# Sixteen expert blocks beside the last batches, with experts in the order of their rows

## What is computed

```python
scores = softmax(xt @ Wg.T)
# the best 2 of 4 groups of 4 experts, then the best 4 experts within them
h = silu(einsum('td,eid->eti', xt, W1)) * einsum('td,eid->eti', xt, W3)
y = einsum('etd,te->td', einsum('eti,edi->etd', h, W2), combine)
z = (silu(xt @ Ws1.T) * (xt @ Ws3.T)) @ Ws2.T
```

## Time and profile before

| | us |
|---|---|
| median of 3 runs | 927.99 |
| profiled execution | 926.76 |
| its span | 924.9 |
| TensorE busy | 774.2 (84%) |
| VectorE busy | 738.9 (80%) |
| GpSimd busy | 517.4 (56%) |
| ScalarE busy | 483.2 (52%) |

### The profile page before, as it was taken

The page is one execution under the profiler, slowest core; times in us unless marked ns, Lnnn a source line. Parts: engine busy times, 40 slices in busy tenths (PEclk is TensorE's granted clock), DMA queues, the critical chain, the costliest instruction groups (busy, mean ns, idle before and its releaser), DMA issues.

```text
span 924.9 us, 20989 instructions
## 1 busy us (share of the span) xinstructions
PE 774.2 (84%) x6103; PEld 692.3 (75%) x6103; DVE 738.9 (80%) x2558; ACT 483.2 (52%) x1236; POOL 517.4 (56%) x512
## 2 busy tenths in 40 slices
PE   3668999999999999999988663899999999999600
PEld 3556788878788878887876552799999999999600
DVE  4556789889998899889967774898888888888534
ACT  4244565645454555555545432666666666666400
POOL 4123334656555655655545473577777777777600
PEclk9779999999999999999999865999999999999855
DMA  3656674567655765567521664978888888888598
GB/s 120 156 145 162 185 195 125 184 193 227 153 185 182 222 170 181 174 193 203 138 77 62 223 242 143 263 149 137 139 139 135 141 137 140 136 136 141 72 377 348
DMA packets 111998, 157.90 MB, mean 171 GB/s; under 512 B 13072, under 2 KB 94992, under 8 KB 111888
## 3 DMA queue, kind: packets, MB, share of 16 engines
q1 hardware_dynamic: 84000, 115.52, 43.0%
q0 software_dynamic: 26736, 36.85, 23.3%
q10 hardware_dynamic: 1152, 4.19, 1.1%
HBM read 74.55 MB, written 81.43 MB: 169 GB/s over the span
## 4 chain that ended last, share of the span: by engine, by line
PE 54%; DVE 22%; issue 9%; DMA 7%; SPq 3%; ACT 2%; POOL 2%; another core or an unknown queue 0%; DVEq 0%; POOLq 0%; ACTq 0%
PE bank L570 25%; PE bank L827 8%; DVE row_max L1121 4%; PE bank L610 4%; PE bank L794 3%; PE bank L614 3%; PE bank L654 3%; DMA acc<-acc_scr 2%; PE bank L638 2%; SPq L551 2%; DMA acc_scr<-yb,token 2%; DVE ropeds_lo L1067 2%; DVE rope_b L1107 2%; PE bank L577 2%; DVE wexp L1067 2%
## 5 line engine op out<-in xcount | busy, mean ns | idle before, releaser
L1534 POOL DMA_INDIRECT acc_scr<-yb,token x143 | 226.3, 1582 | 83.0 <-DMA acc_scr<-yb,token 36.9
L1503 POOL DMA_INDIRECT rows_scr<-xn,rows_of x128 | 128.4, 1003 | 61.9 <-issue 31.1
L570 PE MATMUL bank<-wexp,xbT_hi 128*128 x572 | 151.6, 347 | 4.9 <-DVE xbT_lo L1067 4.3
L1121 DVE TENSOR_REDUCE row_max<-bank 128x2 f32<-128x512 f32 (+1 forms) x192 | 128.9, 682 | 25.9 <-PE bank L614 24.9
L907 ACT ACTIVATE probs<-bank 128x512 f32<-128x512 f32 x192 | 110.7, 607 | 38.9 <-PE bank L654 30.8
L827 PE MATMUL bank<-wexp,upT 112*128 (+1 forms) x572 | 121.5, 305 | 0.3 <-DVE upT L1067 0.2
L610 PE MATMUL bank<-kst,qst 112*128 112x256 f32 (+1 forms) x512 | 98.8, 299 | 23.9 <-DMA kst<-qk_scr 18.8
L610 PEld LDWEIGHTS bank<-kst,qst 112*128 112x128 f32 x512 | 79.4, 199 | 38.8 <-DMA kst<-qk_scr 20.1
L1483 POOL TENSOR_SCALAR_AFFINE_SELECT probs<-probs 128x1024 f32<-128x1024 f32 x64 | 70.2, 1097 | 67.1 <-ACT probs L907 65.9
L570 PEld LDWEIGHTS bank<-wexp,xbT_hi 128*128 128x128 f32 x572 | 94.5, 192 | 7.8 <-issue 7.7
L654 PE MATMUL bank<-qst,kst 114*128 114x512 f32 (+1 forms) x256 | 84.1, 391 | 14.6 <-issue 9.3
(11 more groups left out here) (201 smaller groups left out, 2252.5 us busy)
## 6 DMA issues: line engine op xcount, KB each, us to landing
xb<-rows_scr SPq DMA_DIRECT2D x143, 138.0 KB
qk_scr<-ropeds_hi SPq DMA_DIRECT2D x64, 256.0 KB, 2.5
qst<-qk_scr SPq DMA_DIRECT2D x64, 192.0 KB
kst<-qk_scr SPq DMA_DIRECT2D x64, 192.0 KB
acc<-acc_scr SPq DMA_DIRECT2D x24, 512.0 KB, 14.5
st<-in_wexp SPq DMA_DIRECT2D x16, 608.0 KB
qk_scr<-ropeds_lo SPq DMA_DIRECT2D x32, 256.0 KB, 2.9
acc_scr<-zero SPq DMA_DIRECT2D x10, 768.0 KB
```

The lines of the kernel that those rows point to most:

```text
L570: ins = e.matmul(region, stationary(s, k), moving(m, k), start=(j == 0), stop=(j == n - 1), skip_group_check=True)
L1121: e.tensor_reduce(row_max[:, half, h:h + n, i], view, AX.X, ALU.max).then_inc(s_max)
L1503: e.indirect_dma_start(rows_scr[:, :], bass.IndirectOffsetOnAxis(ap=rows_of[b % 2][:, i, r:r + 1].bitcast(U32), axis=0), x2[:, i, :], None ...
L1534: e.indirect_dma_start(acc_scr[j % NACC][:, :], bass.IndirectOffsetOnAxis(ap=token[j % NW][:].bitcast(U32), axis=0), yb[j % NYB][:], None, ...
```

## The change

The first 16 blocks no longer wait for the list. After batch 12 (ORDER_AT) 13 x 256 x 4 picks have been made, so the expert with most rows has at least 832 of them and thereby six full blocks, the next at least five, then three and two, whatever the data: SURE = [6, 5, 3, 2], AHEAD = 16. A new stage `order` ranks the experts by their counts after batch 12. It has two trips to TensorE and 12 small VectorE instructions, and gives tables `at_slot` (which expert stands in slot x), `slot_row` (where its rows begin) and `slot_w` (where its weights begin). Weights are loaded and kept in this order, so for the 16 blocks the place of the weights in SBUF is known when the program is written, and only row and weight addresses are read from registers, on SyncE.

A new stage `ahead` holds 16 slots of five steps each, which `plan()` lays between the steps of `shared` and `route` of batches 13 to 15. In the resulting order slot 0 begins just before step 20 of batch 15's `mix`, slot 9 ends about where batch 15's `rows_of` are computed (route 23), and slot 15 ends with the tables. GpSimd's add of block j stands in slot j + 6, so two adds (blocks 4 and 5) stand between the eight scatters of batch 15, and ten in all within the stage. When `attend` of batch 15 is done, its three banks join the five. TensorE, ScalarE and VectorE run the same functions for a block as before, now taken step by step.

The list `tables` makes has 127 entries (LISTED) instead of 143. It subtracts what is sure and maps slots to experts, with one more matmul at step 2, one more at step 5 and some more VectorE arithmetic. All 16 tails are cleared in steps 3 to 6 of `tables`, ahead of the first load of the list. Stage `experts` now has four experts and begins at step 10 of `mix` 15 with four loads at once, instead of seven from step 0 on; the other twelve, 24 halves, stand at every third block from 16 to 85, and their loads go out during slots 4 to 7 and then once per six blocks, from block 26 to 68. `st` and `wexp` lie at the end of part two's memory. The adds to `chosen` move from GpSimd to VectorE (route 21 and 22). The start of `tables` and SOONER are shifted.

The core of the diff:

```diff
-SOONER = {"route": [-0.15, -0.3, -0.45]}
+SOONER = {"route": [-0.14, -0.28, -0.42], "shared": [0, 0.0, 0.3]}
...
-    runs += [[B - 1 + 5.2, 0.700 / 8, "tables", B - 1, 8], [0, 0.6 / 10, "load_wqkv", 0, 7], [0.1, 3.4 / 19, "setup", 0, 19],
-             [B - 1 + 2.799, 3.12 / 60, "experts", 0, 1000]]
+    runs += [[B - 1 + 5.46, 1.200 / 8, "tables", B - 1, 8], [0, 0.6 / 10, "load_wqkv", 0, 7], [0.1, 3.4 / 19, "setup", 0, 19],
+             [B - 1 + 2.38, 1.4 / EXPERT_STEPS, "experts", 0, EXPERT_STEPS],
+             [ORDER_AT + 6.1, 0.25 / 6, "order", 0, 6],
+             [B - 1 + 3.77, 2.73 / (5 * AHEAD), "ahead", 0, 5 * AHEAD]]
...
-ON_ATTEND = 7
-EXPERT_STEPS = 5 * ON_ATTEND
-
-BETWEEN = [(h * (E - 1) // (2 * (E - ON_ATTEND)), ON_ATTEND + h // 2, h % 2) for h in range(2 * (E - ON_ATTEND))]
+ORDER_AT = 12
+SURE = [-(-((ORDER_AT + 1) * S * (TOPK - x)) // (E - x)) // P for x in range(TOPK)]
+SLOT_OF = [x for x in range(TOPK) for _ in range(SURE[x])]
+AHEAD = len(SLOT_OF)
+LISTED = NBLK - AHEAD
+EXPERT_STEPS = 5 * TOPK
+BETWEEN = [(AHEAD + 3 * h, TOPK + h // 2, h % 2) for h in range(2 * (E - TOPK))]
...
+            def behind_attention(w):
+                w.wait_ge(s_pv, 4 * B)
+                w.wait_ge(s_oT, 4 * B)
+                w.wait_ge(s_causal, 4 * B)
+                w.wait_ge(s_max, 2 * UNITS * B)
+                w.wait_ge(s_nmax, 2 * B)
...
             def load_expert(x):
                 w.wait_ge(s_wexp, 2 * (x - NST + 1))
-                e.dma_start(st[x % NST][:], a["wexp"][x]).then_inc(d_w[x % NST], 16)
+                w.wait_ge(s_order, ORDERED)
+                at = e.value_load(slot_w[0:1, x:x + 1], min_val=0, max_val=(E - 1) * P)
+                e.dma_start(st[x % NST][:], a["wexp"][bass.ds(at, P), :]).then_inc(d_w[x % NST], 16)
...
+            def load_rows(j):
+                if j < AHEAD:
+                    x = SLOT_OF[j]
+                    w.wait_ge(s_order, ORDERED)
+                    at = e.value_load(slot_row[0:1, x:x + 1], min_val=0, max_val=(E - 1) * CAP)
+                    at = at + (j - SLOT_OF.index(x)) * P
+                    for i in range(NXN):
+                        w.wait_ge(d_rows[i], 128 * len(range(i, ORDER_AT + 1, NXN)))
+                else:
+                    w.wait_ge(s_tab, TAB_ROW)
+                    at = e.value_load(row_t[0:1, j - AHEAD:j - AHEAD + 1], min_val=0, max_val=E * CAP - P)
+                    w.wait_ge(d_tail, 16 * E)
+                    for i in range(NXN):
+                        w.wait_ge(d_rows[i], 128 * (B // NXN))
+                w.wait_ge(s_xb_turned, j - NXB + 1)
+                w.wait_ge(s_picked, j - NXB + 1)
+                e.dma_start(xb[j % NXB][:], rows_scr[bass.ds(at, P), :]).then_inc(d_xb[j % NXB], 16)
...
+            def ahead(k):
+                s, k = divmod(k, 5)
+                if k == 0:
+                    if s == 0:
+                        behind_attention(w)
+                    for j in range(4 if s else 0, 5):
+                        if s + j < AHEAD:
+                            load_rows(s + j)
+                    if 4 <= s < 4 + TOPK:
+                        load_expert(NST + s - 4)
...
+            def block_step(s, k):
+                if k == 0 and s < NBLK:
+                    turn_rows(s)
+                elif k == 1 and 0 <= s - 1 < NBLK:
+                    hidden(s - 1)
+                elif k == 2 and 0 <= s - 2 < NBLK:
+                    turn_hidden(s - 2)
+                elif k == 3 and 0 <= s - 3 < NBLK:
+                    result(s - 3)
...
-            fetch_weights(0)
-            for s in range(NBLK + 3):
...
+            fetch_weights(AHEAD)
+            for s in range(AHEAD, NBLK + 3):
+                for k in range(4):
+                    block_step(s, k)
...
+                elif stage == "ahead":
+                    if k == 0:
+                        w.wait_ge(d_zero, 16 * len(ZEROS))
+                        for i in range(2):
+                            w.wait_ge(d_base[i], 16 * len(range(i, ORDER_AT + 1, 2)))
+                    if k % 5 == 4 and k // 5 >= 6:
+                        add(k // 5 - 6)
...
-            for j in range(NBLK):
...
+            for j in range(AHEAD - 6, NBLK):
+                add(j)
```

More of the change, by code:

```diff
@@ L54 @@
 NXB, NYB, NST, NW = 6, 6, 4, 10
-NTAIL = 4
 NF, TF = 8, 4
@@ L97 @@
     "route": {20: ["rank"]},
+    "order": {0: ["od"]},
+    "tables": {0: ["cb"], 5: ["eb"]},
+    "ahead": {n: u for s in range(18) for n, u in ((5 * s, [f"x{s}"]), (5 * s + 1, [f"h{s - 1}"] if s > 0 else []),
+                                                  (5 * s + 2, [f"t{s - 2}"] if s > 1 else []),
+                                                  (5 * s + 3, [f"y{s - 3}"] if s > 2 else []))},
 }
@@ L106 @@
     "route": {21: ["rank"]},
+    "order": {5: ["od"]},
+    "tables": {5: ["cb"]},
+    "ahead": {n: u for s in range(18) for n, u in ((5 * s + 2, [f"x{s}"]), (5 * s + 3, [f"h{s - 1}"] if s > 0 else []),
+                                                  (5 * s + 4, [f"t{s - 2}"] if s > 1 else []),
+                                                  (5 * s + 5, [f"y{s - 3}"] if s > 2 else []))},
 }
@@ L125, in plan @@
             continue
-        if stage == "experts":
-            if ("attend", B - 1) not in done:
-                continue
+        if stage in ("experts", "ahead", "tables") and ("attend", B - 1) not in done:
+            continue
+        if stage in ("experts", "ahead") and k == 0 and ("order", 0) not in done:
+            continue
+        if stage == "order" and k == 0 and ("ranks", ORDER_AT) not in done:
+            continue
         if stage == "tables" and k == 0 and ("ranks", B - 1) not in done:
@@ L142, in plan @@
             done.add(("ranks", b))
[L143 removed]
+        if run[6] == n:
             done.add((stage, b))
             live.remove(run)
+        if (stage, b, k) == ("attend", B - 1, n - 1):
+            idle += [5, 6, 7]
+            last[5:] = [("attend", b, "scores"), ("attend", b, "scores"), ("attend", b, "out")]
     return order, bank, last
[L150 to L153 removed]
+ORDER_AT = 12
[3 more added lines that the diff above has]
+LISTED = NBLK - AHEAD
+FIRST = [-(-x * (ORDER_AT + 1) * S * TOPK // (E * P)) for x in range(E)]
+EXPERT_STEPS = 5 * TOPK
+BEHIND = 7
+BETWEEN = [(AHEAD + 3 * h, TOPK + h // 2, h % 2) for h in range(2 * (E - TOPK))]
+assert all(FIRST[x] > at for at, x, _ in BETWEEN)
 def layer_kernel(nc, a, out):
@@ L511, in sync_program @@
                     find_tails()
-                    zero_tail(0)
-                    zero_tail(1)
+                elif stage == "tables" and k in (3, 4, 5, 6):
+                    for x in range(4 * (k - 3), 4 * (k - 2)):
+                        zero_tail(x)
+                elif stage == "ahead":
+                    ahead(k)
                 elif stage == "load":
@@ new lines, in tensor_program, with fetch_weights, weights @@
+            at = {}
+            def fetch_weights(j):
+                w.wait_ge(s_tab, TAB_OFF)
+                last = min(j + LOADS, NBLK)
+                for i, reg in enumerate(load_registers(e, "offset", off_t[0:1, j - AHEAD:last - AHEAD])):
+                    at[j + i] = e.snap(reg, min_val=0, max_val=(E - 1) * 2 * WE)
+            def weights(j, m, first, n, rows):
+                if j < AHEAD:
+                    first += (2 * SLOT_OF[j] + m) * WE
+                    return wexp[0:rows, first:first + n]
+                return wexp[0:rows, bass.ds(at[j] + m * WE + first, n)]
@@ new lines, in turn_hidden, with result @@
+            def turn_hidden(j):
+                ps = free_block_bank(w, "t", j, s_upT, j - 1)
+                w.wait_ge(s_up, j + 1)
+                e.transpose(ps[:, 0:P], up[j % 2][:, 0:P], ident[:])
+                e.transpose(ps[:, P:2 * P], up[j % 2][:, IA:IA + 2 * IB], ident[:]).then_inc(s_up_turned)
+            def result(j):
+                ps = free_block_bank(w, "y", j, s_yb, j - 1)
+                w.wait_ge(s_upT, j + 1)
+                hi, lo = upT[j % 2], upT_lo[j % 2]
+                first = [weights(j, m, KT * SI, D, IA) for m in range(2)]
+                rest = [weights(j, m, KT * SI + D, D, P) for m in range(2)]
+                parts = ((hi[0:IA, 0, :], first[0]), (hi[0:IA, 0, :], first[1]), (lo[:], first[0]),
+                         (hi[:, 1, :], rest[0]), (hi[:, 1, :], rest[1]))
+                for n, (left, right) in enumerate(parts):
+                    ins = e.matmul(ps[:, 0:D], left, right, start=n == 0, stop=n == len(parts) - 1,
+                                   skip_group_check=True)
+                ins.then_inc(s_y)
```

501 lines of the change are left out of this document (281 added, 220 removed).

## The result

Four runs of each kernel, on one chip: 940.72 us median after (939.37 to 942.97) against 927.32 before (926.09 to 928.92). **The ratio is 1.0146, 95% interval 1.0117 to 1.0175: 13 us slower where 18 us faster were forecast.** The profiled execution took 939.58 us beside a span of 937.8.

A forecast was written before the change was run, and what follows sets the result against it. Bound: the last batch's chain of small steps, then 2.00 us of TensorE per block left. Block 16 turned at 588 instead of 613, less 7 of extras, gains 18 us: 910 us (903 to 917), range 895 to 925.

The forecast's parts named there:

- e: Extra time in the 126 loop slots after block 16 beyond 2.00 us each, from halves and adds: 7 us.
- 0.15 us a half: Delay taken for each of 24 halves at every third block, 16 to 85: 3.6 us in all.
- the sum: Gain counted from block 16's first transposition to block 142's: 613 - 588 - 7 = 18 us.
- The last x2T: Batch 15's last x2T_lo moves from 533.4 to about 529.4: fewer halves and no weight wait, less the experts' ordering.
- From there to the row numbers: Last x2T_lo to batch 15's row numbers: 33.9 us of VectorE work packed to 0.88 gives 38.5, ready at 568.
- a trough longer than summed: Sign that the forecast is wrong: batch 15's row numbers come beyond 575 us.
- Scatters last, two adds between them, clears under them: After the row numbers: GpSimd's scatters and two adds end at 583, hiding 9 us of clears; rows there at 587.
- Table loads: ScalarE's Silu ahead of batch 15's Exp adds at least two table switches, 2.6 us, mostly covered: 1 us taken.
- X: Start of block 16's first transposition on TensorE, forecast at 588 us.
- The adds, put at 3: GpSimd's adds start the loop six blocks late; the backlog makes TensorE wait 3 us (0 to 25).
- The slower rival: Adds become the loop's bound at 2.43 us each while halves and loads run: 8 us more, 936 us; chance 0.06.
- the blocks ahead only lengthen the trough: Rival: batch 15's chain waits in every queue behind block work, 928 us, no change; chance 0.04.

The follow-up runs named there:

- e9: The kernel before, unedited, on the third chip: 911.82 us, ratio 1.0009 to the kernel before.
- e10: The changed kernel, unedited, on the third chip: 906.07 us, ratio 0.9941 to the kernel before.
- e5: The changed kernel, unedited, on the second chip: 906.84 us, ratio 0.9957 to the kernel before.
- e13: The changed kernel, unedited, on the fourth chip: 907.51 us, ratio 0.9963 to the kernel before.
- e11: Changed kernel with the first eight weight splits three steps later, loads unmoved: 910.39 us, ratio 0.9979 to the kernel before.
- e7: Changed kernel with late blocks, close tables and seven experts, not four, split before the loop: 907.78 us, ratio 0.9961 to the kernel before.
- e16: Changed kernel with late blocks, close tables, seven experts split before the loop, and loop halves cut in two: 900.62 us, ratio 0.9899 to the kernel before.
- e4: Changed kernel with Tanh in place of Silu in the sixteen blocks ahead: 931.19 us, ratio 1.0088 to the kernel before.
- e3: Changed kernel without the loop's 24 halves and their weight loads, all listed blocks using slot 0's weights: 920.11 us, ratio 0.9970 to the kernel before.
- e1: Changed kernel with all steps of the sixteen blocks ahead ordered behind the last batch's ranks: 924.15 us, ratio 1.0006 to the kernel before.
- e2: Changed kernel with the eight tables steps closer together, ahead of most of the last ten block slots: 928.62 us, ratio 1.0062 to the kernel before.
- e8: Changed kernel without nine of eleven TensorE products in each of the sixteen blocks ahead: 903.54 us, ratio 0.9924 to the kernel before.
- e14: Changed kernel without nine of eleven products per block ahead, on the fourth chip: 904.85 us, ratio 0.9945 to the kernel before.
- e17: Changed kernel without nine of eleven products per block ahead, on the fifth chip: 905.46 us, ratio 0.9938 to the kernel before.
- The best form: Changed kernel with loop halves cut in two in neighbouring slots and tables closer together: 897.42 us, ratio 0.9862 to the kernel before.
- e18: Changed kernel with loop halves cut in two and closer tables, on the fifth chip: 898.89 us, ratio 0.9853 to the kernel before.

## Why the prediction was wrong, step by step

Two steps failed. The row numbers were summed with VectorE packed to 0.88 on the way there; it reached 0.63 in the record, where TensorE's results were told late, and 0.80 without that. And e was put at 7 with 0.15 us a half, where it was 12.5 and about 0.5. The term for the last x2T_lo failed too, and is smaller.

The pair e9 and e10 splits the 31.4 us: 11.9 belong to the sum (18 against 6.1), 19.5 to what differed on the chip of the result. Each side is one profile. The unedited changed kernel had its last x2T_lo at 522.31, 520.18 and 523.12 in e5, e10 and e13, so a single mark is known to about 3 us.

**The last x2T, "moves to about 529.4", 4 us earlier.** The step failed: 520.18 against 520.67, 0.5 earlier; and the distance from the x2T_lo ahead of it is 22.5 us in both. The sum took off 2.1 us because ScalarE would no longer meet the first weights in flight. It still does. In e10's last 22.5 us ahead of x2T_lo, waits, and the first split:

```profile
ACT wexp L1098 <- DMA st<-in_wexp: 3.9, 1, 3.9
DVE wexp L1188 <- ACT wexp L1098: 3.0, 1, 3.0
510.92 0.71 ACT L1098 ACTIVATE wexp<-st 128x608 fp32r<-128x608 f32 x1 [3.87 <-DMA st<-in_wexp]
```

VectorE has three halves there and not eight, 2.4 us instead of 6.3, but its busy time is 16.60 us against 18.07 in e9, as other work fills part of the room, and the rest is idle. With the wait for the load at 1.3 us (e11) the distance is 21.8 us, so that wait was worth about 0.7. What the halves themselves cost there stays open: with seven experts again x2T_lo stood 5.1 us later in e7 than in e5, but only 0.7 later in e16 than in e13. On the result's chip x2T_lo came 5.1 us later than before, with a wait of 4.4 for the ordering's late product ahead of it.

**From there to the row numbers, 38.6 us.** 37.6 in e10, but two errors cancel: VectorE was busy 30.2 us, not 33.9, and packed to 0.80, not 0.88. On the result's chip 48.5, with VectorE's work unchanged at 30.5: packed to 0.63. This is the step that failed in the record: it took the packing from a stretch in which TensorE's results came on time, and put waits for late ones at nothing. Without them the agreement is partly luck. The forecast's own sign of a trough longer than summed, row numbers beyond 575, came at 587.

**Scatters last, two adds between them, clears under them.** In e10 the last scatter ended 14.4 us after the row numbers, forecast 15; the 16 clears took 9.0 us under them. The load of block 16 went out 4.5 us after the last scatter, not 1.7. On the result's chip the tables ended 9 us after the scatters, as their steps stood between the late blocks. From x2T_lo to block 16's transposition: 59.2 us in e10, forecast 58.6, in the record 75.5.

**Table loads.** Their number is right: three around batch 15's steps where the kernel before has one, behind them, so two more, 1.28 us each; and Tanh needs none of its own. Their price, forecast 1 in X, is at most 3.6 to 3.9 us in the way by e4, which holds fewer late results as well. The Trainium skill (ScalarE: Activation LUTs, What ACT_TABLE_LOAD costs) has 2.66 us for each switch, 1.28 for the load and the rest a drain. The load in this trace takes those 1.28 us, and no drain shows beside it: in e10 one starts at 535.03, where the copy ahead of it ends at 535.02, and the activation behind it starts at 536.33.

**The extras e = 7.** Mis-sized: 12.5 in the record, 13.6 in e10. The halves take 0.5 us each and not 0.15: VectorE's 5.93 of 6.00 us per three blocks fitted, but the sum over three slots says nothing of one slot, where ScalarE needs 0.37 + 0.32 + 0.39 + 0.47 + 0.70 = 2.25 us with a half and VectorE 1.74 + 0.71 = 2.45, both more than 2.00. The adds, put at 3, take about 1 without halves beside them (e3); with halves, ScalarE waited 2.0 us in all for them between 600 and 740 us in e10. The slower rival had the adds as its bound and so came true in sign alone.

**The kernel before itself** needs 330.3 us from its last x2T_lo to block 142 in e9, against 331.6 in the first profile. These 1.3 us are the rest of the 11.9: 3.5 for x2T, 0.6 for the way to block 16, 6.6 for e, 1.3 here, 12.0.

**The part of the result's chip.** Against e9 and e10, x2T_lo lies 18.3 us later in the changed kernel and 12.7 in the kernel before: 5.6. From there to block 16's xbT_lo it took 76.3 us instead of 60.3: 16.1. Less 1.3 for the kernel before and 0.9 in the loop, that is 19.5. The rival nearest to the record was "the blocks ahead only lengthen the trough" (X at 603, e at 10, a chance of 0.04). That its queue behind block steps carries one late result to all engines is inferred, and fits e1, where the way without blocks in it took 25.6 us.

*Open*: why TensorE's results come late in some executions. Shown is that the long ones begin ahead of the blocks, with the last batches (498 us in the kernel before, 499 in the changed one), that with the blocks late (e1) none comes behind 520 us, though the same block work runs there, that they come with tables, halves and table loads changed (e2, e3, e4) alike, and that the unedited program had none there on three other chips (e5, e10, e13). A low clock alone doesn't call them up: e8 had 0.68 and none. Whether TensorE's own work does was to be told by e14 and e17 and wasn't. The best form was not run on a chip that has them.

## What to carry to other kernels

Work that is interleaved step by step with a latency-bound chain can pay for a disturbance on every in-order queue behind it: cost it by a stretch that is disturbed as well, if there is one, and time it on more than one chip before a per cent is believed. Check a periodic extra by the slot in which it stands, on each engine, not by the mean over its period: cut in two and laid in neighbouring slots, the same work cost 0.2 us a half here instead of 0.5. If an edit takes work off TensorE, look at its granted clock before reading the time. Time saved on an engine ahead of a chain counts only if the chain waited for it.

## What the hardware showed that I had not expected

In the record and in e1 to e4 engines waited up to 4.6 us at a time for products of TensorE whose records had ended; on the four chips of e5 to e18 a profile has at most two remote waits, of 1.7 us in all, in the attention stage. An attention batch took 30.2 us in the record, between 29.4 and 30.5 within one execution in e1 to e4, and 29.4 on the four other chips (29.7 for one batch of the changed kernel). The kernel before took 924 to 927 us there and 911 to 912 here. One change read 1.0146 on the one and 0.9941 to 0.9963 on three of the others, where its interval within one chip is 0.003. The granted clock in the stretch was 0.82 with the late results and 0.95 without; that the lower clock follows from the waits is likely but not shown. With TensorE's work thinned out it was 0.68 (e8), in a stretch as short as that at 0.95.
